# Pixel norms from the Gram diagonal, neighbour norms as shifted DRAM rows, and a longer lag in a convolution loop on one core

## What is computed

```
# convolution block, feature = groupnorm(x)
norm = sqrt(sum(feature * feature, axis=1))
feat_n = feature / maximum(norm, 1e-12)
corr = stack([sum(pad(feat_n, 3)[:, :, r:r+16, c:c+16] * feat_n, axis=1)
              for r, c in offsets])          # 28 offsets, within 3 pixels
x = x + conv_w @ concat([feature, corr]) + conv_b
# attention block, t = tokens of x
q, k, v = ln(t) @ wq, ln(t) @ wk, ln(t) @ wv
t = t + softmax(causal(q @ k.T / sqrt(192))) @ v
# experts
t = t + sum_e dispatch_e * (silu(ln(t) @ W1_e.T) * (ln(t) @ W2_e.T)) @ W3_e.T
```

## Time and profile before

| | us |
|---|---|
| median of three runs | 317.48 |
| the profiled execution | 319.57 |
| its span, first to last instruction | 317.7 |
| busy TensorE / VectorE / ScalarE / GpSimd | 237.5 / 190.8 / 127.3 / 81.4 |

### The profile page before, as it was taken

How to read it: one execution, slowest core, us unless ns; L and a number is a source line. 1 busy time by engine, 2 the same in 40 slices (tenths; PEclk the granted TensorE clock), 3 DMA queues, 4 the chain that set the end, 5 groups by cost and what they waited for, 6 DMA issues and landing times.

```text
span 317.7 us, 5138 instructions
## 1 busy us (share of the span) xinstructions
PE 237.5 (75%) x1354; PEld 217.2 (68%) x1355; DVE 190.8 (60%) x609; ACT 127.3 (40%) x271; POOL 81.4 (26%) x77
## 2 busy tenths in 40 slices
PE   2386798993379698779778574029999999999981
PEld 2285797882268587779678573017898989898971
DVE  2353556533464558777787775844776777776751
ACT  1524046511146779727484311403333333343330
POOL 2211110100000422742635443600222212122222
PEclk9999999997557869665785765557999999999997
DMA  7957712220000040440423401112232000000000
GB/s 270 363 173 215 218 45 76 61 76 13 0 3 0 0 171 12 187 171 25 171 82 141 172 26 38 38 42 62 76 86 77 25 13 25 7 25 25 14 20 0
DMA packets 15712, 25.77 MB, mean 81 GB/s; under 512 B 3879, under 2 KB 12643, under 8 KB 14672
## 3 DMA queue, kind: packets, MB, share of 16 engines
q1 hardware_dynamic: 13824, 22.40, 21.6%
q0 software_dynamic: 1872, 3.18, 2.8%
HBM read 19.50 MB, written 6.76 MB: 83 GB/s over the span
## 4 chain that ended last, share of the span: by engine, by line
PE 60%; DVE 17%; issue 9%; ACT 7%; DMA 3%; POOL 2%; DVEq 0%; POOLq 0%; SPq 0%; ACTq 0%
PE bank L1206 6%; PE bank L955 4%; PE bank L957 4%; PE bank L959 4%; PE bank L956 4%; PE bank L958 4%; PE bank L1182 4%; PE bank L969 3%; PE bank L1207 3%; PE bank L1097 2%; PE bank L950 2%; DVE gst L608 2%; PE bank L1132 2%; PE bank L1197 2%; POOL rn L348 2%
## 5 line engine op out<-in xcount | busy, mean ns | idle before, releaser
L395 POOL DMA_INDIRECT out_rows<-yo,rows x23 | 22.4, 972 | 84.6 <-DVE yo L924 81.1
L373 POOL TENSOR_TENSOR wall<-stage,wall 128x940 fp32r<-128x940 f32 x8 | 17.5, 2186 | 82.2 <-ACT wall L484 82.2
L1206 PE MATMUL bank<-wall,HH 128*128 x92 | 29.4, 375 | 1.5 <-DVE HL L904 1.5
L909 DVE TENSOR_TENSOR gh<-gh,bank 128x470 f32<-128x470 f32 x23 | 14.8, 646 | 22.1 <-PE bank L959 21.2
L568 ACT ACTIVATE HH<-bank 128x512 fp32r<-128x512 f32 x23 | 13.8, 599 | 31.1 <-PE bank L1182 31.1
L1207 PE MATMUL bank<-wall,HL 128*128 x92 | 23.1, 251 | 0.0
L955 PE MATMUL bank<-wall,FH 128*128 x46 | 19.7, 429 | 1.0 <-DVE FL L912 1.0
L904 DVE TENSOR_TENSOR HL<-bank,HH 128x512 fp32r<-128x512 f32 x23 | 15.9, 692 | 7.1 <-ACT HH L568 6.0
L364 POOL DMA_INDIRECT token_rows<-rows,posi x16 | 15.9, 995 | 14.2 <-DVE posi L839 11.0
L574 ACT ACTIVATE FH<-bank 128x256 fp32r<-128x256 f32 x23 | 8.9, 385 | 24.9 <-PE bank L1197 23.5
L1206 PEld LDWEIGHTS bank<-wall,HH 128*128 128x128 f32 x92 | 17.3, 188 | 1.8 <-issue 1.7
(11 more groups left out here) (221 smaller groups left out, 760.2 us busy)
## 6 DMA issues: line engine op xcount, KB each, us to landing
stage<-in_w_all SPq DMA_DIRECT2D x8, 1324.0 KB
rows<-token_rows SPq DMA_DIRECT2D x23, 98.0 KB
near_rows<-gram SPq DMA_DIRECT2D x8, 243.0 KB, 2.6
xcm<-in_x_cm SPq DMA_DIRECT2D x2, 768.0 KB, 8.4
rows<-in_x_tm SPq DMA_DIRECT2D x1, 1536.0 KB, 13.3
token_rows<-emptyt SPq DMA_DIRECT2D x9, 98.0 KB, 5.8
taps_sb<-near_rows SPq DMA_DIRECT2D x8, 103.0 KB, 2.0
small_sb<-in_small SPq DMA_DIRECT2D x1, 704.0 KB, 14.3
```

The costliest lines, as they stand in the source:

```text
L373: nc.gpsimd.tensor_tensor(w[:, W12:2 * W12], stage[:, par, 0:W12], w[:, 0:W12].bitcast(F32), ALU.subtract)
L395: pool.indirect_dma_start(out=out, out_offset=bass.IndirectOffsetOnAxis(ap=rows[:, j, C + 2:C + 3].bitcast(U32), axis=0), in_=yo[:, par], ...
L1206: nc.tensor.matmul(dst[:, 0:2 * C], HH[:, 1 - par, k], w(0, P, c0, c0 + 2 * C), start=(k == 0), stop=False)
```

## The change

1. The pixel norms are taken from the diagonal of the Gram block: VectorE reduces bank x identity over 128x128, once for each half (`pixel_squares`); GpSimd applies the lower bound and the power. `squares`, `pixel_sums`, `spread_norms`, `near_norms`, `copy_norms` are gone.
2. ScalarE takes the Gram block, scaled by the pixel's own norm alone. The neighbours' norms go to DRAM (`norms_to`, 256 numbers into a padded line) and come back as 103 rows shifted by one element each (`norms_from`); GpSimd masks them (`mask_norms`, 103x256), and VectorE multiplies the transposed taps by them (`scale_taps`, in place of ScalarE's copy).
3. `LAG` is 4. Gangs are 1, 3 and 4 images; the first two gangs' factors come ahead of the loop, statistics of the third are spread over passes 0 and 1. VectorE's weight split and the additions are placed anew, GpSimd does `group_shift`'s product, loads are reordered.
4. In attention `nmx` comes out of the reductions directly (negated and scaled, with min for max). `weights_lo` in GpSimd's step t waits for the positions of image t-3 first.

An image now takes four transfers instead of two, and the read of the norms waits in the queue for their write. GpSimd's order in the attention loop is the same rows as before; only the wait is added. The diff, cut to its core:

```diff
-LAG = 3
+LAG = 4
 QUARTER = TILES // 4
-GANGS = ((0, 2), (2, 5), (5, 8))
+GANGS = ((0, 1), (1, 4), (4, 8))
+PADDED = EDGE + PIX + EDGE
...
+            load_images(1)
+            sp.dma_start(s2[:], small2).then_inc(small2_in, 16)
+            load_images(2)
             sp.dma_start(s1[:, conv0:attn0], small1[:, conv0:attn0]).then_inc(small1_in, 16)
-            sp.dma_start(s2[:], small2).then_inc(small2_in, 16)
-            load_images(1)
-            load_images(2)
...
+            def norms_to(b):
+
+                sp.wait_ge(rn_ready, b + 1)
...
+                sp.dma_start(norms[at:at + PIX].rearrange("(h p) -> p h", p=P), rn[:, HALVES * b:HALVES * (b + 1)], allow_slow_non_contiguous=True).then_inc(norms_out[b % 2], 16)
...
+            def norms_from(b):
+
+                sp.wait_ge(norms_out[b % 2], 16 * (b // 2 + 1))
...
+                if b >= 2:
+                    sp.wait_ge(masked, b - 1)
+                window = bass.AP(tensor=norms.tensor, offset=PADDED * b, ap=[[1, REACHED], [1, PIX]])
+                sp.dma_start(rnh[0:REACHED, b % 2], window).then_inc(rnh_in[b % 2], 16)
...
+            for b in range(IMAGES + 1):
+                if b < IMAGES:
+                    norms_to(b)
+                if b:
+                    taps_from(b - 1)
+                if b < IMAGES:
+                    gram_to(b)
+                    norms_from(b)
                 if b < 2:
                     weights_in(b)
-                if b >= LAG:
-                    sp.wait_ge(taps_t_ready, b - LAG + 1)
...
+                pool.wait_ge(gstd_ready, g + 1)
+                nc.gpsimd.tensor_tensor(gnb[:, a:z], mv[:, a:z, :, 0], grs[:, a:z], ALU.mult).then_inc(gnorm_ready, 1)
...
-                pool.wait_ge(ssq_taken, b + 1)
                 at = slice(HALVES * b, HALVES * (b + 1))
+                pool.wait_ge(ssq_ready, b + 1)
+                nc.gpsimd.tensor_scalar(ssq[:, at], ssq[:, at], EPS_NORM * EPS_NORM, None, ALU.max).then_inc(ssq_kept, 1)
+                pool.wait_ge(ssq_kept, b + 1)
                 nc.gpsimd.tensor_tensor(rn[:, at], ssq[:, at], root[:, at], ALU.pow).then_inc(rn_ready, 1)
...
+            def mask_norms(b):
+
+                pool.wait_ge(rnh_in[b % 2], 16 * (b // 2 + 1))
...
+                nc.gpsimd.tensor_tensor(rnm[0:REACHED, b % 2], rnh[0:REACHED, b % 2], c1("beside")[0:REACHED], ALU.mult).then_inc(masked, 1)
...
-            for b in range(IMAGES):
-                pixel_root(b)
-                if b in (0, 2):
-                    group_root(1 + b // 2)
+            group_root(1)
+            for i in range(1, IMAGES + 3):
+                if i == 3:
+                    group_root(2)
+                if i <= IMAGES:
+                    pixel_root(i - 1)
+                if i >= 3:
+                    mask_norms(i - 3)
...
             for t in range(1, IMAGES + 3):
+                if t >= 3:
+                    pool.wait_ge(pos_ready, t - 2 + AHEAD)
                 if t < EXPERTS:
                     weights_lo(t - 1, 1 - t % 2)
...
-            def squares(b):
...
-                nc.scalar.activation(sq[:, b % 2], f32t[:, b % 2], ACT.Square).then_inc(sq_ready, 1)
...
+            def take_gram(b):
+
+                sc.wait_ge(gram_ready, b + 1)
+                sc.wait_ge(rn_ready, b + 1)
...
+                    sc.wait_ge(near_out[b % 2], 16 * (b // 2))
+                for h in range(HALVES):
+                    j, c0 = HALVES * b + h, EDGE * (1 - h)
+                    ins = nc.scalar.activation(gram[:, b % 2, h, c0:c0 + NEAR], bank[4 + b % 2][:, NEAR * h:NEAR * (h + 1)], ACT.Copy, scale=rn[:, j:j + 1])
+                ins.then_inc(gram_taken, 1)
...
+            for i in range(IMAGES + 2):
+                if i >= 2:
+                    take_gram(i - 2)
                 if i < IMAGES:
                     if i in (a for a, _ in GANGS):
                         sc.wait_ge(gnorm_ready, [a for a, _ in GANGS].index(i) + 1)
                     norm_pixels(i)
-                    squares(i)
-                if i == 0:
+                    high_pixels(i)
+                if i == 1:
...
-            def take_gram(b):
-
-                ve.wait_ge(gram_ready, b + 1)
-                ve.wait_ge(rnb_copied, b + 1)
...
-                    ins = nc.vector.scalar_tensor_tensor(out=gram[:, b % 2, h, c0:c0 + NEAR], in0=bank[2 + b % 2][:, NEAR * h:NEAR * (h + 1)],
-                                                         scalar=rn[:, HALVES * b + h:HALVES * b + h + 1], in1=rnb[:, b % 2, q0:q0 + NEAR],
-                                                         op0=ALU.mult, op1=ALU.mult)
...
-                nc.vector.tensor_tensor(spread[:, b % 2], ident.rearrange("p (a q) -> p a q", a=1).to_broadcast(wide),
-                                        rn[:, HALVES * b:HALVES * (b + 1)].rearrange("p (h a) -> p h a", a=1).to_broadcast(wide),
-                                        ALU.mult).then_inc(spread_ready, 1)
...
+                if b >= 2:
+                    ve.wait_ge(gram_ready, b - 1)
...
+            def pixel_squares(b):
+
+                ve.wait_ge(gram_ready, b + 1)
+                ve.wait_ge(small2_in, 16)
+                for h in range(HALVES):
+                    c0 = NEAR * h + (NEAR - P) * h
+                    ins = nc.vector.tensor_tensor_reduce(out=diag[:, b % LAG, h], in0=bank[4 + b % 2][:, c0:c0 + P], in1=ident, scale=1.0, scalar=0.0,
+                                                         op0=ALU.mult, op1=ALU.add, accum_out=ssq[:, HALVES * b + h:HALVES * b + h + 1])
+                ins.then_inc(ssq_ready, 1)
...
+            def scale_taps(b):
+
+                ve.wait_ge(taps_t_ready, b + 1)
+                ve.wait_ge(masked, b + 1)
+                if b >= 2:
+                    ve.wait_ge(conv_ready, b - 1)
+                nc.vector.tensor_tensor(tapsT[:, b % 2], bank[3][0:TAPS, 0:PIX], rnm[0:TAPS, b % 2], ALU.mult).then_inc(taps_copied, 1)
...
+            link(image_stats(0, *GANGS[0]))
             moments(0)
             group_factors(0)
-            group_shift(0)
-            ve.wait_ge(small1_in, 16)
-            ve.wait_ge(wsplit_hi, 1)
-            low_parts(cfH, cfL, c1("cf"), C).then_inc(small_split, 1)
-            for i in range(IMAGES + LAG):
+            link(image_stats(1, *GANGS[1]))
+            moments(1)
+            group_factors(1)
+            for i in range(IMAGES + LAG + 1):
+                if i > LAG:
+                    take_conv(i - LAG - 1)
+                if 1 <= i <= IMAGES:
+                    pixel_squares(i - 1)
+                if LAG <= i < IMAGES + LAG:
+                    scale_taps(i - LAG)
                 if i < IMAGES:
-                    take_squares(i)
-                if 0 <= i - 1 < IMAGES:
-                    take_gram(i - 1)
-                if i < IMAGES:
-                    spread_norms(i)
                     split_pixels(i)
-                if i in (0, 2):
-                    moments(1 + i // 2)
-                    group_factors(1 + i // 2)
-                    group_shift(1 + i // 2)
-                if i == IMAGES:
+                if i in (0, 1):
+                    link(image_stats(2, GANGS[2][0] + 2 * i, GANGS[2][0] + 2 * i + 2))
+                if i == 1:
+                    moments(2)
+                    ve.wait_ge(wsplit_hi, 1)
+                    low_parts(cfH, cfL, c1("cf"), C).then_inc(small_split, 1)
+                if i == 2:
+                    group_factors(2)
+                if i == IMAGES + 1:
                     ve.wait_ge(m_split, 2)
-                    low_parts(mH, mL, bank[7], 2 * CA)
+                    low_parts(mH, mL, bank[2], 2 * CA)
                     low_parts(vwH, vwL, c1("wv"), C).then_inc(attn_split, 1)
-                if i >= LAG:
-                    take_conv(i - LAG)
...
-                    nc.vector.tensor_scalar(nmx[:], smx[:], -SM_SCALE, None, ALU.mult).then_inc(max_ready, 1)
+                    nc.vector.tensor_tensor_reduce(out=sc_sb[:, 0:P], in0=bank[3][:, 0:P], in1=c2("mask")[:, 0:P], scale=-SM_SCALE, scalar=-NEG,
+                                                   op0=ALU.add, op1=ALU.min, accum_out=nmx[:, 0:1])
+                    nc.vector.tensor_tensor_reduce(out=sc_sb[:, P:3 * P], in0=bank[3][:, P:3 * P], in1=c2("mask")[:, P:3 * P], scale=-SM_SCALE,
+                                                   scalar=-NEG, op0=ALU.add, op1=ALU.min, accum_out=nmx[:, 1:2]).then_inc(max_ready, 1)
...
-                    pe.wait_ge(ssq_taken, b)
...
-                        mm = nc.tensor.matmul(bank[5][:, h:h + 1], sq[:, b % 2, t, P * h:P * (h + 1)], one[:, t:t + 1], start=(t == 0), stop=(t == 1))
...
-                nc.tensor.matmul(bank[4][:, 0:PIX], c1("beside"), spread[:, b % 2].rearrange("p h q -> p (h q)"), start=True, stop=True).then_inc(rnb_ready, 1)
...
-            for i in range(IMAGES + LAG):
-                if 0 <= i - 1 < IMAGES:
-                    near_norms(i - 1)
-                if i < IMAGES:
```

(22 more changed lines are left out.)

158 lines of the change are left out of this document (56 added, 102 removed).

## The result

The changed kernel takes 345.96 us (median of 4, 345.35 to 347.42) against 318.29 us (median of 4, 316.16 to 319.42) for the kernel before in the same session: a ratio of 1.089, 95% interval 1.084 to 1.095. The forecast was 286 in 276 to 300. It is slower, in the way of the rival with chance 0.02, and further out than that rival's own 329. Times in this document are medians of all executions, while the ratios leave out executions more than 1.5% above the fastest of their kernel, so that a ratio can differ by up to 1% from the quotient of two medians.

What follows compares the result with a forecast made beforehand. The convolution was taken as a ring through three engines, with VectorE held by GpSimd in attention. Convolution -24.3 and attention -7.0 sum to -31.3 us, put on the median 317.48: 286, range 276 to 300.

Steps and rivals of the forecast that it cites:

- the rival with chance 0.02: Slower: the norm round trip through DRAM eats the gain; at 9 us to landing 329 us in all; chance 0.02.
- the landing of the norm write: Convolution, SyncE queue: norm write lands in 2.3 us, queue time 3.1 an image, under 4.25, so cost 0.
- the cover: Convolution: the norm trip's queue time stays hidden under the 4.25 us image step unless the landing exceeds 3.5 us.
- the break-even: Gain is eaten when convolution ends at 89.6 us: 8.4 us an image on SyncE, 7.6 us to landing.
- that 4.7: Convolution end: 4.7 us added after the last norms are written, in the sum 18+78.4+4.7 = 101.
- the queue rival: Convolution: SyncE's queue is the ring, 5.9 us an image at 5 us to landing, 298 in all; chance 0.12.
- the start: Convolution: image 0's Gram group begins at 13.8 us (before 16.30), image 3's at 28.4 (before 43.81).
- the ring: Convolution at full rate: Gram, handovers, diagonal, scaled taps and split in series, 3.7 us an image, 4.25 with the port.
- The 0.55 for the port: Convolution: split's subtraction on VectorE blocked while GpSimd takes maximum and root, 0.55 us more an image.
- `posi`: Attention: GpSimd's subtractions no longer stall this VectorE cast; 5.0 us of stall go, 4.5 counted; cast 0.17 us.
- `nmx`: Attention: the separate VectorE scaling goes, 4.2 us busy and a semaphore step eight times; 2.5 us counted.
- More comes back: Attention's clock stays up longer, worth up to 6 us, and a free port in convolution 2.6: 277; chance 0.13.

Runs made afterwards that it cites:

- e13: Changed kernel with a 128-row read and the norm write as 128 side-by-side packets of 8 bytes (neighbours' norms wrong): 322.0 us.
- e7: Changed kernel, 103-row read kept, the 256 norms written 64 bytes apart into a tensor nothing reads, zeros read: 315.9 us.
- e14: Changed kernel with a 128-row read, norms written side by side into an own tensor nothing reads, zeros read: 340.2 us.
- e15: As e14, but with the norms written 64 bytes apart: 292.3 us.
- e3: Changed kernel writing two flat rows of 128 ones in place of 256 single norms, 103-row read kept: 313.4 us.
- e4: Changed kernel with two flat rows of ones written and 128 rows read in place of 103: 293.1 us.
- e5: Changed kernel with only the SyncE queue order changed, each norm read put behind the next pass's sheared read: 351.5 us.
- e1: Changed kernel without the norms' DRAM write and read, mask multiplied with ones, neighbour's norm missing: 281.8 us.

## Why the prediction was wrong

**The step that failed** is the landing of the norm write: "No row has 4-byte pieces. Nearest are `near_rows`, 2.6 us to landing, and `taps_sb`, 2.0 ... I take 2.3, bounds 2.0 and 5". It measured 10.4. The rest of that step was right as a mechanism: the cover was said to be gone above 3.5, and the break-even put at 7.6 us (e13 with a landing of 8.2 is 1% slower than the kernel before, e7 with 6.7 is 1% faster). Its own formula, 0.4 + landing + 0.4 for an image, gives 11.2 at 10.4 us: the last norms would have landed at 18 + 89.6 = 107.6 (109.6 measured, images 1 and 2 with 15 us each and the later ones with about 10), and 4.7 more give 112, where the last addition ended at 120.8. Most of the rest is in that 4.7, which took 11.2: the last 103-row read took over 6 us from its issue (109.63) to the mask (115.88), and TensorE's granted clock was 0.50. Two things were wrong in the choice of rows. Those rows have pieces of 412 and 972 bytes, and the write has 4; e14 and e15 show that distance decides, 9.8 against 3.7. And the upper bound "twice the slower, chosen by me" wasn't a bound: nothing in the trace held the price down. The rival that the step named got 0.02 on "no row of this size lands that late", which is no evidence where no row has that form. The rule quoted there (the Trainium skill, DMA: Bandwidth & Descriptors, Specifications: pieces under 512 B are read, modified and written) spoke for the upper side. Size alone isn't it here: 412-byte pieces landed in 2.0 us and 4-byte pieces 64 bytes apart in 3.7. No run shows whether reading and writing back is what makes near pieces wait.

**Also missed: the 103-row read.** "Pieces are only 16 an engine" was said against the queue rival. For the read it is false, all 103 went over one engine; behind a mended write it costs 20 us (e3 to e4).

**A claim on contention.** The near rows and taps were taken at their old landings with new transfers around them. They land in 10.0 and 9.8, and the one other order tried doesn't help (e5).

**Right, by e1 and the changed kernel:** the start (14.17 for 13.8; image 3 at 26.88 for 28.4), the end of the convolution without the trip (57.4 for 58.3), and so the mechanism of that part of the gain. The whole comes to e1's 281.8 against 286, the difference being mostly the attention part. The mean step at full rate was 4.28 for 4.25, but that is partly luck: it is made of other parts than the ring that was added up. The 0.55 for the port had the split held beside the maximum and the root; there the split kept its 0.68, and GpSimd's maximum was lengthened instead (0.92). VectorE was held in other places (the split 0.92 and a cast 0.81 beside the mask), and two of the three steps had waits for taps or ScalarE that the sum left out. The Trainium skill (SBUF — State Buffer, SBUF: two separate sides) says that whichever of the pair starts first gets the port for its whole instruction and the other blocks fully. The split at 35.73, behind the mask's start, agrees. The maximum at 39.21 doesn't: by the trace it began 0.17 us before the split and yet was the one held, and so at 30.15 (0.96); the measurement decides.

**Attention** gave 12.4 for 7.0. `posi` was right in size (5.5 for 4.5, the cast 168 ns for 0.17 us). `nmx` was mis-sized: 2.5 counted, about 7 measured. It stands in front of ScalarE's exponential, whose wait for it fell by 5.7 us with the fold, and the granted clock of the stage rose from 0.68 to 0.79 over both edits. That was the first half of the rival "More comes back"; what the clock alone gave isn't separated.
